# Softmax denominators from VectorE block transposes and sums in place of TensorE products over ones

## The reference, cut to what matters

```python
def _L0_attn_b_ref(x_q, w_q, w_k, w_v, w_o):          # x_q (4, 1024, 256), 16 heads of 64
    q = jnp.einsum('ntc,hdc->nhtd', x_q, w_q)
    k = jnp.einsum('ntc,hdc->nhtd', x_q, w_k)
    v = jnp.einsum('ntc,hdc->nhtd', x_q, w_v)
    a = jnp.einsum('nhtd,nhsd->nhts', q, k) / math.sqrt(q.shape[3])
    a = jnp.where(causal_forbidden[None, None], -jnp.inf, a)
    a = jax.nn.softmax(a, axis=3)
    y = jnp.einsum('nhts,nhsd->nthd', a, v).reshape(a.shape[0], t, -1)
    return y @ w_o
...
x = x + _L0_attn_a_ref(_layernorm(x))      # mixes the 16 parts of each row
x = x + _L0_ffn_ref(_layernorm(x), ...)    # 8 experts, each takes its top 256 tokens
x = x + _L0_attn_b_ref(_layernorm(x), ...)
x = x + _L0_ffn_ref(_layernorm(x), ...)
return x
```

## Time and profile before

| | us |
|---|---|
| median of 3 runs | 2243.05 |
| the runs | 2241.84 to 2243.07 |
| span of the profiled execution, first to last instruction | 2235.8 |
| time of the profiled execution itself | not listed; the runs lie 6.0 to 7.3 above the span |
| TensorE busy, matmuls | 2149.9 (96%) |
| VectorE busy | 1465.4 (66%) |
| ScalarE busy | 1003.6 (45%) |
| GpSimd busy | 1368.7 (61%) |
| TensorE's mean granted clock | 0.987 of full speed |

### The profile page before, as it was taken

How to read it: one execution, slowest core, us unless ns; L and a number is a source line. 1 busy time by engine, 2 the same in 40 slices (tenths; PEclk the granted TensorE clock), 3 DMA queues, 4 the chain that set the end, 5 groups by cost and what they waited for, 6 DMA issues and landing times.

```text
span 2235.8 us, 34077 instructions
## 1 busy us (share of the span) xinstructions
PE 2149.9 (96%) x12130; PEld 1597.8 (71%) x12130; DVE 1465.4 (66%) x3349; ACT 1003.6 (45%) x1907; POOL 1368.7 (61%) x1237
## 2 busy tenths in 40 slices
PE   6998999999999999999999999999999899999997
PEld 5455788889876666766657666667666588889997
DVE  6365688675757666467674577874877636975553
ACT  4411553444445545345553354542554425434443
POOL 2322676677537776566674576664677846777774
PEclk9899999999999999999999999999999999999999
DMA  4432544555432212212312222221220244545552
GB/s 132 144 129 86 151 117 111 151 144 137 114 88 67 51 36 76 67 52 73 76 48 67 67 78 56 58 61 54 76 76 21 76 132 115 140 113 139 134 144 29
DMA packets 145048, 206.04 MB, mean 92 GB/s; under 512 B 19432, under 2 KB 112112, under 8 KB 144880
## 3 DMA queue, kind: packets, MB, share of 16 engines
q1 hardware_dynamic: 120304, 170.30, 25.4%
q0 software_dynamic: 24576, 33.57, 8.8%
HBM read 130.03 MB, written 39.85 MB: 76 GB/s over the span
## 4 chain that ended last, share of the span: by engine, by line
PE 73%; DVE 9%; issue 4%; POOL 4%; ACT 2%; DMA 1%; SPq 1%; POOLq 0%; DVEq 0%; ACTq 0%
PE psum L1299 12%; PE psum L1320 11%; PE psum L1446 11%; PE psum L1348 7%; PE psum L1411 7%; PE psum L1427 6%; PE psum L1471 5%; PE psum L1362 4%; PE psum L1376 3%; PE psum L1456 3%; POOL t_acc L2390 2%; DVE f_hlo L2134 1%; DVE f_hhi L2132 1%; PE psum L1389 1%; PE psum L1267 1%
## 5 line engine op out<-in xcount | busy, mean ns | idle before, releaser
L1713 ACT ACTIVATE t_p<-psum 128x512 f32<-128x512 f32 (+3 forms) x768 | 323.6, 492 | 294.3 <-PE psum L1427 284.6
L2390 POOL TENSOR_TENSOR t_acc<-t_acc,t_p 128x1024 f32<-128x1024 f32 (+3 forms) x256 | 416.9, 1629 | 14.5 <-ACT t_p L1713 0.5
L2309 POOL TENSOR_TENSOR f_wlo<-f_wst,f_whi 128x256 fp32r<-128x256 f32 x256 | 221.8, 922 | 150.6 <-ACT f_whi L1646 150.6
L1320 PE MATMUL psum<-f_whi,f_hhi 128*128 128x256 f32 x1024 | 294.9, 288 | 6.2 <-DVE f_hlo L2134 6.1
L1446 PE MATMUL psum<-t_p,t_v 128*64 128x512 f32 (+3 forms) x1536 | 288.8, 496 | 7.3 <-POOL t_p L2370 7.3
L1320 PE MATMUL psum<-f_whi,f_hlo 128*128 128x256 f32 x1024 | 289.4, 283 | 0.0
L1320 PE MATMUL psum<-f_wlo,f_hhi 128*128 128x256 f32 x1024 | 289.2, 282 | 0.0
L2132 DVE CAST f_hhi<-f_h 128x512 fp32r<-128x512 f32 x256 | 141.9, 554 | 208.0 <-ACT f_h L1664 153.2
L1664 ACT ACTIVATE f_h<-psum 128x512 f32<-128x512 f32 x256 | 153.0, 598 | 275.8 <-PE psum L1299 246.8
L1411 PE MATMUL psum<-t_qa,t_ka 128*128 128x512 f32 (+3 forms) x768 | 222.7, 370 | 1.8 <-DVE t_mx L2180 0.6
L2390 POOL TENSOR_TENSOR t_acc<-t_p 128x768 f32<-128x768 f32 x64 | 134.6, 2103 | 136.4 <-PE psum L1456 133.1
(11 more groups left out here) (288 smaller groups left out, 4408.1 us busy)
## 6 DMA issues: line engine op xcount, KB each, us to landing
f_wst<-in_L_ffn_w SPq DMA_DIRECT2D x64, 1024.0 KB
t_ka<-t_ka SPq DMA_DIRECT2D x64, 256.0 KB, 3.3
t_qb<-t_qa SPq DMA_DIRECT2D x64, 256.0 KB, 4.0
t_wk<-wkT SPq DMA_DIRECT2D x32, 256.0 KB, 4.0
t_wq<-wqT SPq DMA_DIRECT2D x32, 256.0 KB, 4.0
t_wv<-wvT SPq DMA_DIRECT2D x16, 512.0 KB, 4.9
normal<-f_xy SPq DMA_DIRECT2D x5, 1024.0 KB, 10.3
a_x<-in_L_attn_a_x SPq DMA_DIRECT2D x4, 1024.0 KB, 10.0
```

The costliest lines, as they stand in the source:

```text
L1320: m = pe.matmul(out, h[:, js], w[:, f, :], start=(f == 0 and a == 0 and j % 2 == 0), stop=(f == FT - 1 and a == 2), skip_group_check=True)
L1713: act.activation(p[:, i, q0:], k.bank[bank][:, q0:], ACT.Exp, scale=1.0 / float(np.sqrt(k.DH))).then_inc(k.drained[bank], 1)
L2309: m = pool.tensor_tensor(t["wlo"][n % 2][:, i, ks], t["wst"][:, i, ks], t["whi"][n % 2][:, i, ks].bitcast(F32), ALU.subtract)
L2390: pool.tensor_tensor(acc[:, :, q0:], (p0 if kt == 1 else acc)[:, :, q0:], p[:, :, q0:], ALU.add).then_inc(k.p_acc, 1)
```

## The change

The sum over the partitions is made in another way. A new step, `fold_sums`, runs on VectorE at the start of the pair in which `divide` stands. It transposes `acc` in blocks of 32 x 32, all 1024 columns at once, into a new tile `turned`. In it, each group of 32 columns of a partition belongs to one query and to one of the four groups of 32 keys. A sum over each group of 32 columns gives `part`, 128 x 32: for each head 16 columns. What is left is a sum over four partitions that lie 32 apart, and that is what the product in `divide` now does: its weights are `fold`, a constant matrix with a one wherever the two indices agree modulo 32, 64 columns wide, and it has 16 columns moving for each head instead of 512. Its result is already in the blocked form of which the reciprocal is taken, so the transpose from PSUM goes (`sum_rows` is the reciprocal alone, straight from the bank).

`divide` moves behind the pair's `weigh` and waits for `part`. The tile `den` becomes a half of `turned`, so a fold waits until GpSimd has scaled the chunk before. The first addition into an `acc` waits for the fold's transpose instead of the product. Two small sums on VectorE build `fold` at the start.

```diff
@@ class Kernel
-        self.d_den = Marks(s("dve_den"), "reciprocal", "rows")
+        self.d_den = Marks(s("dve_den"), "turned", "part", "rows")
...
+        self.fold = c("fold", [P, self.DH])
...
-        t["den"] = [sb("t_den", [P, BANK]) for _ in range(2)]
+        t["turned"] = sb("t_turned", [P, 2 * BANK])
+        t["den"] = [t["turned"][:, c * BANK:(c + 1) * BANK] for c in range(2)]
+        t["part"] = sb("t_part", [P, 2 * BANK // 32])
@@ attention
+        def fold(n):
+
+            if ends(n - 3):
+                self.fold_sums(*pairs[n - 3][:2])
+
         def finish(n):
 
-            if ends(n - 3):
-                self.divide(*pairs[n - 3][:2])
             if 0 < n <= len(pairs):
                 u, c, kt = pairs[n - 1]
                 self.weigh(u, c, kt)
                 self.weigh(u, c, kt + 1)
             if ends(n - 3):
+                self.divide(*pairs[n - 3][:2])
                 self.sum_rows(*pairs[n - 3][:2])
...
                 u, c, kt = pairs[n]
+                fold(n)
                 sums(n, 0)
@@ TensorE.divide
+        n = BANK // 32
         bank = self.take(("den", u, c), self.work_bank())
-        self.wait_ge(k.p_acc, k.sum_count(u, c, k.KPC * (c + 1) - 1))
+        self.wait_ge(k.d_den.sem, k.d_den.at(2 * u + c, "part"))
         for i in range(2):
-            m = pe.matmul(k.bank[bank][i * DH:(i + 1) * DH, :], k.ones[:, 0:DH], t["acc"][(2 * u + c) % 2][:, i, :],
+            m = pe.matmul(k.bank[bank][i * DH:(i + 1) * DH, 0:n], k.fold[:], t["part"][:, i * n:(i + 1) * n],
                           start=True, stop=True, skip_group_check=True)
@@ VectorE.constants
+        for n in range(0, k.DH, 32):
+            dve.tensor_reduce(k.fold[:, n:n + 32], k.ident[:].rearrange("p (g d) -> p d g", d=32), AX.X, ALU.add)
@@ VectorE
+    def fold_sums(self, u, c):
+
+        k, dve, t = self.k, self.e, self.k.t
+        chunk = 2 * u + c
+        self.wait_ge(k.p_acc, k.sum_count(u, c, k.KPC * (c + 1) - 1))
+        if chunk:
+            self.wait_ge(k.p_yt, chunk)
+            self.wait_filled(("den", (chunk - 1) // 2, (chunk - 1) % 2))
+        dve.transpose(t["turned"][:], t["acc"][c][:].rearrange("p i q -> p (i q)")).then_inc(k.d_den.sem, 1)
+        self.wait_ge(k.d_den.sem, k.d_den.at(chunk, "turned"))
+        dve.tensor_reduce(t["part"][:], t["turned"][:].rearrange("p (n j) -> p n j", j=32), AX.X,
+                          ALU.add).then_inc(k.d_den.sem, 1)
+
     def sum_rows(self, u, c):
...
-        den = t["den"][c]
-        if chunk > 1:
-            self.wait_ge(k.p_yt, chunk - 1)
-        dve.transpose(den[:], k.bank[bank]).then_inc(k.drained[bank], 1)
-        self.wait_drained(("den", u, c))
-        dve.reciprocal(t["rden"][chunk % 2][:, :], den[:].rearrange("p (n j) -> p n j", j=32)[:, :, 0]
-                       ).then_inc(k.d_den.sem, 1)
+        dve.reciprocal(t["rden"][chunk % 2][:, :], k.bank[bank][:, 0:BANK // 32]).then_inc(k.drained[bank], 1)
@@ GpSimd.add_up
             if u:
-                self.wait_filled(("den", u - 1, c))
+                self.wait_ge(k.d_den.sem, k.d_den.at(2 * (u - 1) + c, "turned"))
```

More of the change, by code:

```diff
@@ L423 @@
     xt_block = qk_load = v_load = qk_product = qk_low = qk_double = v_product = skip
-    row_max = part_max = max_rows = high_scores = scores = weigh = add_up = divide = sum_rows = scale_rows = skip
+    row_max = part_max = max_rows = high_scores = scores = weigh = add_up = skip
+    fold_sums = divide = sum_rows = scale_rows = skip
     values_done = out_weights = out_load = out_product = out_add = skip
@@ L1004, in units @@
             for n in range(4):
+                fold(len(pairs) + n)
                 sums(len(pairs) + n, 0, 1)
@@ L2211, in scale_rows @@
         chunk = 2 * u + c
-        self.wait_ge(k.d_den.sem, k.d_den.at(chunk, "reciprocal"))
-        dve.transpose(t["den"][c][:], spread(t["rden"][chunk % 2][:], 2, 32)).then_inc(k.d_den.sem, 1)
+        self.wait_drained(("den", u, c))
+        dve.transpose(t["den"][c], spread(t["rden"][chunk % 2][:], 2, 32)).then_inc(k.d_den.sem, 1)
     def out_add(self, b, c, n):
@@ L2403, in scale_rows @@
         self.wait_ge(k.a_pvs, chunk + 1)
-        pool.tensor_tensor(t["yT"][c][:, hp, :], t["pvs"][chunk % 2][:], t["den"][c][:],
+        pool.tensor_tensor(t["yT"][c][:, hp, :], t["pvs"][chunk % 2][:], t["den"][c],
                            ALU.mult).then_inc(k.p_yt, 1)
```

## The result

The changed kernel takes 2264.39 us in the median of 4 runs (2257.42 to 2266.77) against 2242.45 for the kernel before (4 runs, 2241.39 to 2243.07): a ratio of 1.0096, 95% interval 1.0084 to 1.0109. It is slower, by 21.9 us; I had said 2246.5 with slower as the likeliest sign. The time lies 17.9 us above the forecast and 0.4 us above the end of the range. The profiled execution after took 2266.77 us, with a span of 2265.3 against 2235.8.

The account below looks back on a forecast made before the run. The prediction took TensorE's queue to bound attention. Its terms, -58.2 + 17.9 + 28.8 + 6.4 + 2.5 + 4.2 + 2.0, gave +3.6 us on 2243.05, stated as 2246.5 us, range 2228 to 2264.

Parts of the forecast that it names:

- What leaves and what comes to TensorE: At 64 denominator places, old products over ones leave TensorE's queue (-58.2 us) and four small passes each come (+17.9 us).
- a case without any wait: Fold ready when the value products end, so all stalls go: -40.3 us on the span, 2203 us.
- The fold's price and the waits: VectorE's fold takes 2.47 us; TensorE waits 28.8 us at 512-key chunks, 6.4 and 2.5 at some 1024-key chunks.
- What lies behind the fold: VectorE's later maxima free PSUM banks late for TensorE's scores: 4.2 us over 28 units, 2.0 in the four worst.
- the second place: Pair 4 of each unit, denominators of its own 512-key chunk: 1.03 us wait, +0.40 us net, plus 0.15 for banks.
- the first: Pair 2 of each unit, denominators of the previous unit's 1024-key chunk: mostly no wait, a clean gain of 0.63 us.
- GpSimd's wait: GpSimd's 133 us wait before its first sum of a 1024-key chunk would move to VectorE's transpose and shrink.
- any wait put into it lengthens the span one for one: In attention TensorE's queue is the time, so each wait added there costs exactly its own length.
- The signs named for being wrong: Fold under 2.2 or over 2.8 us, small pass over 0.1, or bank waits at the scores up over 10 us.
- The wait does not come: Rival: the fold is ready when TensorE's value products end; 2203 us in full, 2233 for half; chance 0.24 under 2238.5.
- The products are not cheaper: Rival: a 16-column TensorE pass costs 0.111 us, 0.44 a place, raising the time to 2257 us; chance 0.12.
- VectorE becomes the bound: Rival: late VectorE maxima delay the next unit's scores, 1 us in 16 to 32 units, 2262 to 2278 us; chance 0.16.

Follow-up runs that it names:

- e2: Changed kernel with the small products reading a constant without waiting, and the fold replaced by two one-element copies on VectorE: 2186.34 us, ratio 0.9784 to the kernel before.
- e1: Changed kernel with the small products reading constant ones, so not waiting for the fold, which VectorE still makes: 2264.82 us, ratio 1.0127 to the kernel before.
- e10: Changed kernel with the fold only for the 32 512-key chunks, old products over ones for the 1024-key chunks: 2263.86 us, ratio 1.0117 to the kernel before.
- e8: Changed kernel with the fold only for the 32 1024-key chunks, old products over ones for the 512-key chunks: 2234.90 us, ratio 0.9980 to the kernel before.
- e3: Changed kernel with two useless products over ones (0.91 us) ahead of the value products at each 512-key chunk's place: 2252.52 us, ratio 1.0076 to the kernel before.
- e9: Changed kernel with the fold only at 28 1024-key chunks, those covered by value projections, old products elsewhere: 2220.95 us, ratio 0.9920 to the kernel before.
- e4: Changed kernel with a head-by-head fold, the 512-key chunk's standing one pair earlier, ahead of four maxima: 2274.97 us, ratio 1.0162 to the kernel before.
- e5: Changed kernel with a head-by-head fold in its old place and the denominator product one pair later: 2335.83 us, ratio 1.0445 to the kernel before.
- e7: Changed kernel with a head-by-head fold behind the short maxima and the denominator product one pair later: 2398.97 us, ratio 1.0724 to the kernel before.
- e0: The changed kernel run again, unchanged: 2256.92 us (2251.28 to 2266.59, 6 runs), ratio 1.0095 to the kernel before.

## Why the prediction was right in sign and 18 us short in size

*What leaves and what comes to TensorE (-58.2, +17.9).* Right in kind; e2 shows both together, -48.2 against my -40.3 for a case without any wait. The small pass was priced too high (0.28 a place; 0.18 in e1, and 0.22 where it follows a wait), 4 to 6 us in the change's favour.

*The fold's price and the waits (2.47; +28.8, +6.4, +2.5).* Right: 2.46, and 33.7 us of waits in 37 times, 28 of them alike as forecast. They cost a little more than the idle time shown, since the queue's step before them ends 0.1 us ahead of the modelled end.

*What lies behind the fold (+4.2, +2.0).* Right in size, 5.5 us, and in kind. Ordinary units without a low stretch take 32.32 to 32.36 us after, 32.34 before: the whole mechanism nets nothing there, as the sum said (+0.40 - 0.63 + 0.15 a unit). Its parts were both too small, and cancel: by e10 the second place costs 0.77, not 0.55, and by e8 the first gives 0.78, not 0.63. Why the second place costs 0.2 more is open. GpSimd's wait did not move to VectorE's transpose, as I had said, but to ScalarE's weights (114.7 us).

*All together.* By the table 24.7 us were added from the first score to the end, 22.2 of them low clock. That leaves +2.5 where the sum has +3.6. That they lie so close is in part luck, by the cancelling just shown.

*The term that was missing.* The prediction priced a wait of TensorE as its length. The step that failed is "any wait put into it lengthens the span one for one": here it costs its own length and then, behind about a third of the 37 waits, a stretch at 1.2 GHz, which takes 1.6 us from a unit (33.95 to 33.99 us with one, 32.32 to 32.36 without). Behind the fold's waits that is 23.9 us, in place of a term that the sum had at nothing. The signs named for being wrong (the fold, the small pass, the bank waits) all stayed away, since none of them looked at the clock. The rows for it were in the trace before, at 1135.49 and 1137.00 to 1140.50, and I read the clock only as the mean of 0.99 in the earlier trace rows. e3 bears it out by putting work where the wait was, e8 against e9 by taking away four waits. (The Trainium skill's page "TensorE: Matmul & The Clock Gate" tells of such a case, of another kernel, in its section "A second HAM failure mode: psum-queue depth-cycling": small idle times between groups of products make the clock swing between its two levels, and each swing is paid. The trace agrees, with 0.53 granted behind a wait of 0.9 us. I cited that page for a price and passed over this section; it gives no price for a swing.)

*The rivals.* "The wait does not come" is out, by 33.7 us of it. "The products are not cheaper" is out, by 0.18 a place. "VectorE becomes the bound" gave 2262 to 2278 and the time fell there, but not by its mechanism: it priced late banks at 16 to 32 us, and they are 5.5, and VectorE still waits for TensorE ahead of the negated maxima (72.5 us in 27 times, 46.3 in 25 before). In e1, e4, e5 and e7 late banks do become the wait, once the fold pushes the maxima instead of the product.

*The run's own shift.* 4.8 us of the profiled difference arose ahead of the attention, in code that is the same but for two small sums; 3.4 of them are low clock there (18.8 us up to 640 against 15.4). The medians (21.9 apart) and the table from the first score (24.7, one execution each) are the two measures of what the change costs.

*What stays open.* Which waits are followed by the lower clock: of the first units after, those at 672.7 and 705.0 have the same 0.90 us of wait and no low stretch, the four from 737.4 on have one each. The length counts (none behind 0.4 to 0.6 us, three of four behind 1.5 and more, in e0 and e8 too), but among equal waits of 0.9 us no run here settles it: 9 of 28 after, 12 of 28 in e0, 5 of 28 in e10. e3 against e0 shows only that without the waits most of the stretches, and the scatter between runs, go.

## What to carry to other kernels

Price a wait that is put into a full TensorE queue at more than its length: look in the trace before for the granted clock after the few waits that are there, and charge it. An engine that is idle for a quarter of the time can still have no room at the place where the new work must stand: ask who is queued behind it, and take the new form only at places where it is covered (here 28 of 64, for 0.8% gained instead of 1% lost). To find whose wait it is, take away the work, not only the wait: e1 moved the wait two instructions on, e2 removed it.

## What the runs showed of the hardware

- The lower clock often comes late: the wait ends at 737.38, TensorE then runs at full clock to about 739, and drops while it is fully busy, until about 742.5. Before, the wait ends at 1135.49 and the lower clock lies from 1137.0 to 1140.5. Behind the twelve waits for the fold the distance is 0.6 to 2.8 us. Waits of 0.9 us (737.38, granted 0.53 behind it) and of 2.2 us (1135.49, 0.51 behind it) were both followed by it. In a longer wait it comes inside: before, it falls at 1765.1, with TensorE idle since 1762.1, and eight value passes take 3.25 us:

```profile
1766.56 3.25 PE L1446 MATMUL psum<-t_p,t_v 128*64 128x512 f32 x8 [4.50 <-POOL t_p L2370]
```
- Putting 29 us of useless products in front of the waits did not lengthen the time (median 4.4 us lower, the intervals overlap), raised the mean clock (0.974 to 0.981 in e0, 0.982 to 0.983 in e3), and cut the scatter over runs from 15 to 3 us (e3 against e0).
- Passes of 16 columns with 64 columns of weights go at 0.045 us each (0.18 for four, e1). A 32x32 transpose of 1024 fp32 columns takes 1.237 us, a sum of 1024 fp32 elements a lane 1.220.
